# Gated cross-attention and expert layer: router products and context scores in four column groups, scores by way of memory

## The reference, cut to what matters

```python
si = einsum('bnd,d->bn', ctx, W[0, :256]); sj = einsum('bnd,d->bn', ctx, W[0, 256:])
mix = 0.6 * sigmoid(si[:, :, None] + sj[:, None, :] + b[0]) + 0.4 * layernorm(x)
x = x + tanh(g_xattn) * mix
xt = layernorm(x).reshape(4096, 1024)
logits = xt @ wg                       # 1024 x 8
idx = argmax(softmax(logits)); gate = softmax(logits)[idx]
y[n] = gate[n] * (W_e[idx[n]] @ xt[n] + b_e[idx[n]])
out = x + tanh(g_ffn) * y
```

## Time and profile before

| | us |
|---|---|
| median of three runs | 683.54 |
| lowest and highest | 682.17, 690.35 |
| span of the profiled execution | 687.3 |
| busy in it: PE, DVE, ACT, POOL | 576.6, 445.2, 274.1, 331.8 |

### The profile page before, as it was taken

The page is one execution under the profiler, slowest core; times in us unless marked ns, Lnnn a source line. Parts: engine busy times, 40 slices in busy tenths (PEclk is TensorE's granted clock), DMA queues, the critical chain, the costliest instruction groups (busy, mean ns, idle before and its releaser), DMA issues.

```text
span 687.3 us, 14019 instructions
## 1 busy us (share of the span) xinstructions
PE 576.6 (84%) x2841; PEld 461.2 (67%) x2842; DVE 445.2 (65%) x557; ACT 274.1 (40%) x408; POOL 331.8 (48%) x489
## 2 busy tenths in 40 slices
PE   7898889888707969979779997995999799699990
PEld 5576667666505848858567885884888588588870
DVE  3357778697699885856784587588378557843420
ACT  2367766686424333413333333333343233333220
POOL 1446777788623336325336533633633364356540
PEclk8569999999957989989989998997999899899995
DMA  7911577576679876764776497577756656545530
GB/s 262 403 40 33 175 261 237 198 217 223 239 258 259 238 214 190 225 208 152 224 220 196 147 243 213 189 219 215 217 168 204 189 166 198 164 132 186 182 126 13
DMA packets 83666, 134.72 MB, mean 196 GB/s; under 512 B 11568, under 2 KB 64304, under 8 KB 83504
## 3 DMA queue, kind: packets, MB, share of 16 engines
q1 hardware_dynamic: 73712, 99.47, 49.4%
q0 software_dynamic: 9792, 33.82, 12.8%
HBM read 99.44 MB, written 35.91 MB: 197 GB/s over the span
## 4 chain that ended last, share of the span: by engine, by line
PE 27%; DVE 23%; issue 19%; ACT 9%; POOL 7%; DMA 6%; DVEq 3%; POOLq 2%; ACTq 2%; SPq 1%
PE pair L1058 12%; DVE wt L782 7%; PE pair L985 4%; DVE xr L718 4%; ACT wt L598 4%; DVE pair L777 4%; PE pair L996 3%; PE pair L969 3%; PE pair L974 3%; ACT rb L617 2%; DVE rows L804 2%; DMA out_x<-rows,scatter_row 2%; DMA rows<-table 1%; DVE xc_tr L725 1%; POOL out_x L500 1%
## 5 line engine op out<-in xcount | busy, mean ns | idle before, releaser
L1058 PE MATMUL pair<-wt,xt 128*128 x1728 | 416.2, 404 | 62.6 <-DVE rows L804 41.6
L1058 PEld LDWEIGHTS pair<-wt,xt 128*128 128x128 f32 x1728 | 336.9, 196 | 141.5 <-issue 66.5
L488 POOL TENSOR_TENSOR rows<-rows,rb 128x1024 f32<-128x1024 f32 x37 | 88.7, 2398 | 164.2 <-ACT rb L617 162.6
L782 DVE TENSOR_TENSOR wt<-pair,wt 128x1024 f32 (+1 forms) x64 | 77.5, 1212 | 32.7 <-ACT wt L598 32.7
L598 ACT ACTIVATE wt<-pair 128x1024 f32 (+1 forms) x64 | 64.2, 1024 | 77.7 <-DVE pair L777 70.1
L604 ACT ACTIVATE xt<-pair 128x1024 fp32r<-128x1024 f32 x38 | 39.0, 1026 | 133.0 <-DVE pair L790 110.6
L777 DVE STREAM_TRANSPOSE pair<-w_raw 128x1024 f32<-128x1024 f32 x64 | 79.7, 1250 | 1.9
L790 DVE STREAM_TRANSPOSE pair<-xb 128x1024 f32<-128x1024 f32 x38 | 47.7, 1255 | 46.5 <-issue 26.3
L804 DVE SCALAR_TENSOR_TENSOR rows<-pair,scal,rows 128x1024 f32<-128x1024 f32 x36 | 46.0, 1278 | 44.6 <-PE pair L1058 44.2
L617 ACT ACTIVATE rb<-bias_bc,scal 128x1024 f32 (+1 forms) x37 | 46.0, 1244 | 48.4 <-POOL scal L485 41.1
L794 DVE TENSOR_TENSOR xt<-pair,xt 128x1024 fp32r<-128x1024 f32 x38 | 46.4, 1221 | 28.1 <-ACT xt L604 25.9
(11 more groups left out here) (123 smaller groups left out, 417.9 us busy)
## 6 DMA issues: line engine op xcount, KB each, us to landing
w_raw<-in_L_ffn_W SPq DMA_DIRECT2D x256, 128.0 KB
xb<-table SPq DMA_DIRECT2D x156, 128.0 KB
rows<-table SPq DMA_DIRECT2D x38, 520.0 KB
xr<-in_x SPq DMA_DIRECT2D x32, 512.0 KB, 6.9
ctx_in<-in_ctx SPq DMA_DIRECT2D x8, 512.0 KB, 4.9
bias_bc<-in_L_ffn_b SPq DMA_DIRECT2D x8, 512.0 KB
out_x<-rows,scatter_row POOLq DMA_INDIRECT x36, 4.2
table<-xr,pos POOLq DMA_INDIRECT x32, 4.5
```

The source lines that it names most:

```text
L488: nc.gpsimd.tensor_tensor(rows[:, k, 0:H], rows[:, k, 0:H], rb[:, :], ALU.add).then_inc(base_ready, 1)
L782: nc.vector.tensor_tensor(where[:, :, 1].rearrange("p a k o -> p (a k) o"), ps[:, :].rearrange("p (k o) -> p k o", k=K), where[:, :, 0].re ...
L1058: last = nc.tensor.matmul(out_ps[r % 2][:, HALF * h:HALF * (h + 1)], xt[:, r % RING, x_part, k, :], wt[:, bass.ds(par, 1), w_part, k, HALF ...
```

## The change

Router products: `wg_sb` is 32 columns wide with zeros behind the eight, and block k of a tile goes to column group k mod 4, which writes partitions 32j to 32j+31 of PSUM; each group sums two blocks. The logits copy takes all 128 partitions, and the product that turns logits to tokens uses `fold`, a sum of four identity blocks, in place of the identity, so that it adds the four partial sums. Context scores: both weight vectors, halved, are columns 0 and 1 of `wij`; tile c of a group goes to column group c; ACT reads the 128 x 128 result with a quarter of the bias and stores it to memory by a DMA of its own; SP loads the sj rows back broadcast over the partitions and si in eight pieces as columns (`load_scores`). The context is read in other row order, in pieces of 1 KB. ACT copies the whole turned tile, DVE none of it. The context groups are turned at tiles 0, 2, 4, 8, 12 and 16 and summed one tile later, and SP's loads stand in a new order.

```diff
-    ctx_t = ctx.rearrange("b (p a c) d -> b a p (c d)", a=TB // GR, c=GR)
+    ctx_t = ctx.rearrange("b (a c p) d -> b a p c d", a=TB // GR, c=GR)
...
+    ctx_rows = nc.dram_tensor("ctx_rows", [NG * P, P], F32, kind="Internal").ap()
+    by_kind = ctx_rows.rearrange("(x r) n -> r x n", r=CG)
...
+        def ctx_sum(g):
+            return ctx_home(g)[:, 0:P]
+
+        def ctx_turn_tile(g):
+
+            return 2 * (g - 2) if g < 4 else GR * (g - 3)
...
+            def load_context(g):
+                sp.dma_start(ctx_in[:, g % 2, :].rearrange("p (c d) -> p c d", c=GR),
+                             group_of(ctx_t, g)).then_inc(ctx_landed[g % 2], 16)
+
+            def load_tile(t):
+                sp.dma_start(xr[:, slot_of(t), 0:H], tile_of(x_t, t)).then_inc(x_landed[slot_of(t)], 16)
+
+            def next_context(g):
+                sp.wait_ge(ctx_turned, g - 1)
+                load_context(g)
+
+            def next_tile(t):
+                sp.wait_ge(row_stored[slot_of(t)], 16)
+                load_tile(t)
+
+            def load_scores(b):
+                for k in range(2):
+                    sp.wait_ge(sums_stored[k], 16 * (b + 1))
+                if b >= 2:
+                    sp.wait_ge(th_ready, TB * (b - 1))
+                sp.dma_start(sj[:, b % 2, :, :], by_kind[1, TB * b:TB * (b + 1), :].unsqueeze(0)
+                             .to_broadcast([P, TB, P])).then_inc(sj_landed[b % 2], 16)
+                with nc.allow_non_contiguous_dma(reason="8 numbers a row"):
+                    for c in range(TB):
+                        sp.dma_start(si_half[P // TB * c:P // TB * (c + 1), TB * b:TB * (b + 1)],
+                                     by_kind[0, TB * b + c, :].rearrange("(i k) -> i k", k=TB)).then_inc(
+                                         si_landed[b % 2], 16)
+
...
+            next_context(2)
+            next_context(3)
+            sp.wait_ge(zeros_ready, 1)
+            sp.dma_start(wg_sb[:, :, 0:E], wg.rearrange("(k p) e -> p k e", p=P)).then_inc(wg_landed, 16)
             for t in range(4, 8):
-                sp.dma_start(xr[:, t, 0:H], tile_of(x_t, t)).then_inc(x_landed[t], 16)
-            for g in (2, 3):
-                sp.wait_ge(ctx_turned, g - 1)
-                sp.dma_start(ctx_in[:, g % 2, :], group_of(ctx_t, g)).then_inc(ctx_landed[g % 2], 16)
+                load_tile(t)
+            load_scores(0)
             for t in range(8, RX):
-                sp.dma_start(xr[:, t, 0:H], tile_of(x_t, t)).then_inc(x_landed[t], 16)
+                load_tile(t)
             sp.dma_start(bias_bc[:, 0, :], bias[0:1, :].to_broadcast([P, H])).then_inc(bias_landed, 16)
+            next_context(4)
+            next_context(5)
+            load_scores(1)
+            next_context(6)
+            for t in range(RX, RX + 2):
+                next_tile(t)
+            next_context(7)
+            for t in range(RX + 2, RX + 5):
+                next_tile(t)
+            load_scores(2)
+            for t in range(RX + 5, RX + 12):
+                next_tile(t)
+            load_scores(3)
+            for t in range(RX + 12, T):
+                next_tile(t)
...
-            for g in range(4, NG):
-                sp.wait_ge(ctx_turned, g - 1)
-                sp.dma_start(ctx_in[:, g % 2, :], group_of(ctx_t, g)).then_inc(ctx_landed[g % 2], 16)
-            for t in range(RX, T):
-                sp.wait_ge(row_stored[slot_of(t)], 16)
-                sp.dma_start(xr[:, slot_of(t), 0:H], tile_of(x_t, t)).then_inc(x_landed[slot_of(t)], 16)
...
+            nc.gpsimd.memset(wij[:, :, :], 0.0)
+            link(nc.gpsimd.memset(wg_sb[:, :, :], 0.0))
+            pool.sem_inc(zeros_ready, 1)
...
+            link(nc.gpsimd.tensor_tensor(fold[:, :], ident[:, 0:E], ident[:, CG:CG + E], ALU.add))
+            for j in range(2, NCG):
+                link(nc.gpsimd.tensor_tensor(fold[:, :], fold[:, :], ident[:, CG * j:CG * j + E], ALU.add))
+            pool.sem_inc(masks_ready, 1)
...
             def context_copy(g):
                 act.wait_ge(ctx_turned, g + 1)
                 if g > 1:
-                    act.wait_ge(si_summed, g)
+                    act.wait_ge(ctx_summed, g)
                 nc.scalar.activation(ctx_turned_home(g).rearrange("p c d n -> p (c d n)"), ctx_home(g)[:, :],
                                      ACT.Copy).then_inc(ctx_copied, 1)
 
             def context_sums(g):
-                act.wait_ge(sj_summed, g + 1)
-                nc.scalar.activation(
-                    sj[:, (g // 2) % 2, :, GR * (g % 2):GR * (g % 2 + 1)].rearrange("p n c -> p c n"),
-                    sj_sum(g), ACT.Identity, bias=gates[:, 2:3]).then_inc(sj_ready, 1)
-                act.wait_ge(si_summed, g + 1)
-                nc.scalar.activation(si_half[:, GR * g:GR * (g + 1)], si_sum(g), ACT.Copy, scale=0.5).then_inc(si_ready, 1)
+                act.wait_ge(ctx_summed, g + 1)
+                if g >= 2:
+                    act.wait_ge(sums_stored[g % 2], 16 * (g // 2))
+                nc.scalar.activation(ctx_sums[:, g % 2, :], ctx_sum(g), ACT.Identity,
+                                     bias=quarter_b[:, 0:1]).then_inc(sums_ready, 1)
+                act.wait_ge(sums_ready, g + 1)
+                act.dma_start(ctx_rows[P * g:P * (g + 1), :], ctx_sums[:, g % 2, :]).then_inc(sums_stored[g % 2], 16)
 
             def half_tanh(t):
                 b = t // TB
-                act.wait_ge(sj_ready, 2 * b + 2)
-                act.wait_ge(si_ready, t // GR + 1)
+                if t % TB == 0:
+                    act.wait_ge(sj_landed[b % 2], 16 * (b // 2 + 1))
+                    act.wait_ge(si_landed[b % 2], 16 * TB * (b // 2 + 1))
                 act.wait_ge(mv_ready, t + 1)
                 if t >= RTH:
                     act.wait_ge(xc_ready, t - RTH + 1)
                     act.wait_ge(sq_ready, t - RTH + 1)
-                nc.scalar.activation(th[:, t % RTH, :], sj[:, b % 2, :, :].rearrange("p n c -> p (n c)"),
-                                     ACT.Tanh, bias=si_half[:, t:t + 1], scale=0.5,
+                nc.scalar.activation(th[:, t % RTH, :], sj[:, b % 2, :, :].rearrange("p c n -> p (c n)"),
+                                     ACT.Tanh, bias=si_half[:, t:t + 1],
                                      accum_out=xr[:, slot_of(t), TH:TH + 1]).then_inc(th_ready, 1)
 
...
             def copy_turned(t):
-                act.wait_ge(xc_turned[0], t + 1)
+                act.wait_ge(xc_turned, t + 1)
                 if t >= 2:
                     act.wait_ge(routed, t - 1)
-                nc.scalar.activation(xc_tr[:, t % 2, 0:K // 2, :].rearrange("p k n -> p (k n)"),
-                                     xt_ps[t % 2][:, 0:HALF], ACT.Copy).then_inc(xc_copied[0], 1)
+                nc.scalar.activation(xc_tr[:, t % 2, :, :].rearrange("p k n -> p (k n)"),
+                                     xt_ps[t % 2][:, :], ACT.Copy).then_inc(xc_copied, 1)
 
...
             for g in range(2):
                 context_copy(g)
+            act.wait_ge(wij_ready, 2)
             for g in range(2):
                 context_sums(g)
             for t in range(RTH - 1):
                 half_tanh(t)
-            context_copy(2)
-            context_sums(2)
             for t in range(T):
                 g, r = t // GR, t % GR
                 if t + RTH - 1 < T:
...
                     logits_copy(g - 1)
                 square(t)
                 copy_turned(t)
-                if r == 0 and g + 3 < NG:
-                    context_copy(g + 3)
-                if r == 2 and g + 3 < NG:
-                    context_sums(g + 3)
+                for n in range(2, NG):
+                    if ctx_turn_tile(n) == t:
+                        context_copy(n)
+                    if ctx_turn_tile(n) + 1 == t:
+                        context_sums(n)
 
...
-            for c in range(DC):
-                last = nc.vector.tensor_copy(wj_bc[:, c, :], wcol[:, DC + c:DC + c + 1].to_broadcast([P, P]))
-            last.then_inc(wj_ready, 1)
+            dve.wait_ge(zeros_ready, 1)
+            nc.vector.tensor_scalar(wij[:, :, 0:2], wcol[:, :].rearrange("p (a c) -> p c a", c=DC), 0.5, None,
+                                    ALU.mult).then_inc(wij_ready, 1)
+            dve.wait_ge(gates_landed, 48)
+            nc.vector.tensor_scalar(quarter_b[:, :], gates[:, 2:3], 0.25, None, ALU.mult).then_inc(wij_ready, 1)
...
-            def copy_turned(t):
-                dve.wait_ge(xc_turned[1], t + 1)
-                if t >= 2:
-                    dve.wait_ge(routed, t - 1)
-                nc.vector.tensor_copy(xc_tr[:, t % 2, K // 2:K, :].rearrange("p k n -> p (k n)"),
-                                      xt_ps[t % 2][:, HALF:2 * HALF]).then_inc(xc_copied[1], 1)
...
-                copy_turned(t)
-                if t + LEAD < T:
                     moments(t + LEAD)
...
             def sum_context(g):
+
                 pe.wait_ge(ctx_copied, g + 1)
```

(52 more changed lines are left out.)

52 lines of the change are left out of this document (26 added, 26 removed).

## The result

The changed kernel takes 715.09 us (median of 3 runs, 710.5 to 720.04) against 683.54 before: a ratio of 1.049, interval 1.037 to 1.062. The profiled execution spans 713.0 us (before: 687.3). So the loss is 31.6 us by the medians and 25.7 us in the profiled pair, because the profiled execution of the kernel before was longer than its median; the traces can explain only the 25.7. Ratios, here and in the experiments, leave out executions more than 1.5% longer than the fastest of their kernel, while the medians beside them keep them, so the two can differ a little.

What follows compares the result with a forecast made beforehand. The first stage was taken as bound by a ring of PE and DVE work, with POOL next at 17.2 us a group; 3.8, 12.9 and 2.2 us won made 18.9, so 683.5 - 19 = 664.5 us, range 653 to 681.

Steps and rivals of the forecast that it cites:

- The trip, 11.4 us, at most 15.4: Scores through memory: store lands 4.5 us, nine issues on SP 3.9, last landing 3; 11.4 us in all.
- By batch: Score waits on ACT: first tanh near 24.5 us; batch 1 about 6 exposed, batch 2 1.5, batch 3 nothing.
- The sum: First stage: 3.8 us won to linear 9, 12.9 to linear 31, 2.2 in the tail; 18.9 won, span 668.4.
- Routing 0.8 us: Router products on PE in four column groups: 0.8 us a tile instead of 1.91, between 0.5 and 1.91.
- The first rival, no overlap: Column groups on PE don't overlap, routing stays at 1.91 us: 14 us won, 669.5; chance 0.12.
- ACT's and PE's costs: Per tile or context: ACT's copy 1.02 us, context read 0.3, DMA issue 0.5; PE's context sums 0.8.
- POOL sets the pace, 17.2 us a group from tile 9: Middle of the first stage: POOL works without pauses, 17.2 us a group; linear 9 to linear 31 takes 96 us.
- The slow rival: Trip exposed before tanh 8, 16 and 24 on ACT: 50.7 us of waits, 24 slower, 707.5; chance 0.08.
- the clock rival: Short routings let PE's clock fall, turns take 1.97 us, not 1.09: 6 us lost and 3 around, 673.5; chance 0.12.
- The tail, 2.2 won: End of the first stage: last add to last logits copy takes 4.4 us instead of 6.6.
- The loop, 485: Expert loop after the first stage: code unchanged, keeps its length of 485 us.
- the 183 of the forecast: Handover from first stage to expert loop: first load of expert rows near 183 us, before 202.22.

Runs made afterwards that it cites:

- e15: e3 with batch 0's scores loaded ahead of x tiles 6 and 7, batch 2's ahead of tile 20, and 16 unread products a tile on PE: 671.22 us, 0.973.
- e3: Changed kernel with the scores' memory ordered by kind, sj read in one 4 KB piece a partition and si in one load: 679.14 us, 0.987.
- e12: e11 with 16 unread bf16 products a tile on PE: 677.12 us, 0.983.
- e11: e3 with batch 0's scores loaded from ACT's own queue and batch 2's ahead of x tile 20: 683.31 us, 0.993.
- e5: e3 with 16 unread bf16 products a tile on PE, save where a context is turned: 675.25 us, 0.987.
- e10: e3 with the routing's products one after another into 8 partitions, as before the change, instead of column groups: 686.46 us, 0.997.
- e2: Changed kernel with one load of si per batch in place of eight, sj loaded as in the changed kernel: 700.38 us, 1.022.
- e16: e3 with si in the eight small loads of the changed kernel instead of one: 686.2 us, 0.997.

## Why the prediction was wrong

- *The trip, 11.4 us, at most 15.4.* This is the step that failed, in two of its terms. Batch 0: the store takes 4.54 us, as forecast (4.5). The nine issues take 7.0 instead of 3.9. The last landing takes 11.0 instead of 3. The trip is 22.3 us. I sized the landing by its 512 bytes ("this small one"), below the 6.9 of an x tile, though it stands behind a 512 KB transfer in 1024 pieces, whose kind has the longest median landing in the kernel, 13.3 us. And 0.43 an issue came from four loads at the handover; eight small ones took up to 11.6, 1.45 each on average.
- *By batch.* First tanh at 38.22, not 24.5 (bounds 22 to 28). Batch 1: 9.0 us exposed, at the far end of 3 to 10. Batch 2: 13.75, not 1.5: the load that waits for row 4's store came first, as forecast (SP reaches the scores at 104.79), but from there to tanh 16 it takes 19.7 us, 11.6 of them in the eight issues. Batch 3: 6.33, not none; the forecast counted its lead of 21 us from row 11, but what came last was the store of context 7's sums, and from its issue (147.16) to the point where ACT wants the scores (159.35) lie 12.2 us.
- *The sum.* That is 13.7 + 3.0 + 12.3 + 6.3 = 35.3 us more than counted. With 18.9 us to win this makes 16.4 lost; 24.6 are. The other 8.2 lie in the terms beside these waits. Linear 9 ends at 81.8 instead of 64.3 (17.5 later, 16.7 of it the waits), linear 9 to linear 31 takes 118.7 instead of 96 (22.7 more, 18.6 of it the waits), and from there to the handover it takes 26.4, where the 25.3 of before less 2.2 were forecast (3.3 more). So 0.8, 4.1 and 3.3 us are pace and tail. The clock of 0.63 is a candidate for the middle; no run holds it in the changed kernel itself.
- *Routing 0.8 us.* Right: 0.64 in a row of its own, 1.0 at 1.2 GHz. The first rival, no overlap, is refuted. By the Trainium skill (TensorE: Matmul & The Clock Gate, Part 3) weight loads overlap running products only where row groups differ. The trace differs: these groups share all 128 rows, and the routing's 16 weight loads, none shorter than 106 ns, lie within 0.38 us, beside 16 products in 0.64. Nor does a pause stand in front of it: the product before it ends at 145.56, after the routing's first has begun (145.49).
- *ACT's and PE's costs.* Right: copy 1.00 to 1.03 (1.02), context read 0.37 (0.3; the ratio named for it gives 0.14, a quarter of 0.575), DMA issue 0.33 (0.5), context sums 0.77 (0.8).
- *POOL sets the pace, 17.2 us a group from tile 9.* Not in the changed kernel, where POOL waits for tanh. In e15 it does, at 17.0. But it takes the held clock too: e3's last four groups take 18.2 on average (iotas from 75.16 to 148.07), e15's 17.0 (73.16 to 141.20). So the clock rival came true beside the other: turns of 1.97 us came back (at 130.62 us in the chain). Its size in the changed kernel wasn't measured; in the repaired ones the held clock goes with 2.2 us (e12 against e11) to 5.4 (e5 against e3) from first tanh to handover, less than the 9 it was given.
- *The tail, 2.2 won.* From the start of the last add (204.36) to that of the last logits copy (209.92) it takes 5.6 us, before 6.6: 1.0 won, with a last turn of 1.98 us at 1.2 GHz where 1.1 was counted. From the last iota to the handover nothing is won (41.88 us, before 41.84); in e15 it is 39.87, 2.0 won.
- *The loop, 485.* Right: 486.2.
- *The slow rival.* It came true: its mechanism, its place, its sign. It was priced at 707.5 and is 715.1, and at 24 us lost against 24.6 in the traces. That nearness is luck: it counted 50.7 us of waits before tanh 8, 16 and 24, where 29.1 were measured, and left out batch 0, which carries 13.7 us, and the 8.2 us of pace and tail. Its chance of 0.08 rested on leads counted in tiles against a trip of 11.4 to 15.4 us, where batch 0's took 22.3.

With the layout of the trip repaired, e3 hands over at 189.38, 6 us later than the 183 of the forecast, nearly all of it between linear 9 and linear 31 (102.1 us, forecast 96). Only e15, which adds another order of loads and products that hold the clock, meets the forecast, and there term by term: linear 9 ends at 62.6 (64.3), linear 31 is 95.9 us later (96), the handover at 181.07, and the span is 666.4 us (668.4). So POOL's pace and the tail were sized well for a held clock, which the changed kernel doesn't have.

## What to carry to other kernels

Price a new trip through memory by its worst transfer, and for that count the pieces into which each load is cut and the issues that stand ahead of the last one, not only its bytes; then lay the data out so that a partition reads one piece. Compare the whole trip with the lead in microseconds at the new pace, not in tiles at the old one. And when products on PE get shorter, look at the granted clock of the stage: here the time that PE no longer needed for routing came back in part as slower turns (369 ns a product in e3 against 279 in e10). Last, when the starts of two traces differ by a few us, compare first what the same code does in both: here one store took 2.8 to 8.9 us.

## What the runs showed of the hardware

- Four column groups that share all rows run side by side: 16 fp32 passes of 128 columns took 0.64 us instead of 1.91, with full-height turns before and after. A turn's product took 279 ns beside ungrouped routings (e10) and 291 beside grouped ones (e15), both at a clock of 0.96.
- A load to 128 partitions of 4 KB each landed in 5.4 us (median) in one piece a partition (e3) and in 12.5 us in pieces of 512 bytes that lie 16 KB apart (e2).
- Eight loads of 512 bytes held the issuing queue for 3.67 to 5.38 us in company of 4 KB pieces (e16) and for 4.33 to 11.60 in company of 512-byte pieces (changed kernel).
- One 64 KB store, issued near 16.5 us behind the same code, landed after 2.80 us in e12 and after 8.93 us in e11.
- Shorter routings on PE went with a lower clock, 0.71 of 2.4 GHz from 102 to 143 us (e3) against 0.96 (e10), and 16 unread bf16 products a tile with 0.92 (e5).
